# Slot attention stage of a transformer kernel: the first stage's instructions in another order

## What is computed

```python
q = _rope(x @ Wq); k = _rope(x @ Wk); v = x @ Wv          # x is the layer norm of the input
sk = clip(x @ sk_w1 @ sk_w2 + sk_b2, -32, 32)             # low rows (16), then slots' logits (4 x 64)
sv = clip(x @ sv_w1 @ sv_w2 + sv_b2, -32, 32)
wk = exp(sk); zk = cumsum(wk)
S = where(mask, q @ k.T, 0)
p = softmax(S @ wk * scale / zk)
wv = exp(sv); zv = cumsum(wv)
A = where(mask, (p / zv) @ wv.T, 0)
o = A @ v
g = x @ Wg
on = o * rsqrt(mean(o * o) + EPS) * gnorm_w
return x + (on * g * sigmoid(g)) @ Wo
```

## Time and profile before

| what | us |
|---|---|
| median of 3 runs | 1717.63 |
| lowest and highest of them | 1714.06, 1718.74 |
| the profiled execution's own time | 1717.68 |
| its span, first to last instruction | 1715.9 |
| of it the first stage | 306 |

### The profile page before, as it was taken

The page is one execution under the profiler, slowest core; times in us unless marked ns, Lnnn a source line. Parts: engine busy times, 40 slices in busy tenths (PEclk is TensorE's granted clock), DMA queues, the critical chain, the costliest instruction groups (busy, mean ns, idle before and its releaser), DMA issues. The chain is left out here.

```text
span 1715.9 us, 37883 instructions
## 1 busy us (share of the span) xinstructions
PE 1520.5 (89%) x14142; PEld 731.0 (43%) x14142; DVE 1189.5 (69%) x1931; ACT 1256.8 (73%) x2113; POOL 529.5 (31%) x908
## 2 busy tenths in 40 slices
PE   7899997784699999998889999968874999999998
PEld 4676665662133333336633333345541333333256
DVE  4677778798999999966710000048878999999743
ACT  4555553597488888885679999925763888888863
POOL 3432342552323333334400000013212233333362
PEclk9899989797699999999989999989986999999999
DMA  4000000025534343320133333201333333333211
GB/s 132 1 1 1 1 1 1 1 78 156 155 97 110 108 112 107 109 64 27 38 94 95 96 100 97 68 24 49 99 106 113 84 90 92 87 93 93 67 38 38
DMA packets 140410, 125.42 MB, mean 73 GB/s; under 512 B 38410, under 2 KB 118340, under 8 KB 140228
## 3 DMA queue, kind: packets, MB, share of 16 engines
q1 hardware_dynamic: 130980, 121.90, 23.9%
q0 software_dynamic: 8192, 0.77, 0.9%
q10 hardware_dynamic: 1056, 0.33, 0.1%
HBM read 77.19 MB, written 44.96 MB: 71 GB/s over the span
## 5 line engine op out<-in xcount | busy, mean ns | idle before, releaser
L1700 ACT ACTIVATE m_probs<-m_psum 128x512 f32<-128x512 f32 (+1 forms) x768 | 511.7, 762 | 63.1 <-PE m_psum L1623 62.2
L1700 ACT ACTIVATE e_probs<-e_psum 128x512 f32<-128x512 f32 x512 | 276.3, 596 | 53.3 <-PE e_psum L1623 51.8
L1740 DVE TENSOR_REDUCE a_minus_max<-m_psum 128x2 f32<-128x1024 f32 x256 | 300.9, 1219 | 14.3 <-PE m_psum L1632 13.0
L1740 DVE TENSOR_REDUCE a_minus_max<-e_psum 128x2 f32<-128x1024 f32 x256 | 300.6, 1219 | 14.4 <-PE e_psum L1632 13.0
L1623 PE MATMUL m_psum<-m_q_stack,m_k_stack 114*32 114x512 bf16 (+1 forms) x4096 | 295.8, 385 | 6.7 <-DMA m_k_stack<-n_parts 4.6
L1643 PE MATMUL m_psum<-m_probs,m_v_ones 128*32 128x512 f32 x2048 | 271.0, 602 | 3.4 <-DVE m_pair L1690 2.1
L1623 PEld LDWEIGHTS m_psum<-m_q_stack,m_k_stack 114*32 114x32 bf16 (+1 forms) x4096 | 106.9, 96 | 225.8 <-issue 126.2
L1623 PE MATMUL e_psum<-e_q_stack,e_k_stack 126*32 126x512 bf16 x2048 | 157.8, 385 | 2.2 <-ACT e_probs L1700 2.2
L1643 PE MATMUL e_psum<-e_probs,e_v_ones 128*32 128x512 f32 x1024 | 132.2, 593 | 0.0
L1632 PE MATMUL m_psum<-m_k_stack,m_q_stack 48*128 48x512 bf16 x512 | 93.0, 400 | 32.0 <-DVE a_minus_max L1740 24.4
L1632 PE MATMUL e_psum<-e_k_stack,e_q_stack 60*128 60x512 bf16 x512 | 93.9, 400 | 27.9 <-DVE a_minus_max L1740 22.6
(11 more groups left out here) (401 smaller groups left out, 2648.1 us busy)
## 6 DMA issues: line engine op xcount, KB each, us to landing
polar_q<-m_late SPq DMA_DIRECT2D x24, 256.0 KB, 3.0
polar_k<-m_late SPq DMA_DIRECT2D x24, 256.0 KB, 3.4
m_q_stack<-polar_q SPq DMA_DIRECT2D x64, 96.0 KB, 2.3
m_k_stack<-polar_k SPq DMA_DIRECT2D x64, 96.0 KB, 2.4
ctx<-a_context_pairs SPq DMA_DIRECT2D x48, 128.0 KB
a_context_pairs<-slot_w SPq DMA_DIRECT2D x24, 256.0 KB, 2.2
m_q_stack<-dist_parts SPq DMA_DIRECT2D x192, 32.0 KB
m_k_stack<-dist_parts SPq DMA_DIRECT2D x192, 32.0 KB
```

The lines of the kernel that those rows point to most:

```text
L1700: act.activation(self.buf.probs[(NT * m + c) % self.buf.PROBS][:, self.WIDE * part:self.WIDE * (part + 1), :], self.ps_s[i % self.PAIRS], ...
L1740: dve.tensor_reduce(self.minus_max[n % 2][:, k:k + NT + 1:NT], self.ps_r[r % self.TWOS], AX.X, ALU.max, negate=True).then_inc(self.two_fre ...
```

## The change

`gate_sigmoid` is cut into three methods, one for each activation, and the lists of PE, ACT and DVE are written in another order, with the banks' plan to match. On PE: `low` goes between the two `slot_logits`; the projections of tiles 3 and 2 follow those of 1 and 0 directly, ahead of `mean_squares` and `project_out`; `slot` 1 and 0 end the step with `gate` behind them; `slot` 2, `key_sums` 0 and `slot` 3 begin the next. The gate moves from bank 5 to bank 4, behind the contexts `o` and ahead of `xnT`. On ACT the four activations of the gate go into the next step, one by one between the copies for scores and `weights` 3. On DVE `clip` 1 and 0 come behind `apply_rms`, `scan` 1 ends the step ahead of `clip` 2, the statistics of the next sequence come earlier, and `gate_product` comes behind the second `state_copy`. POOL's list stays as it is. No operation is added or dropped.

```diff
-            ("slot2", 2, 1, ...), ("slot3", 3, 1, ...), ("zk0", 5, 1, ...),
+            ("slot2", 2, 1, ...), ("zk0", 5, 1, ...), ("slot3", 3, 1, ...),
...
-            ("low", 4, 0, ...), ("gT", 5, 0, (slot.gated_ready,)), ("slot1", 1, 0, ...), ("slot0", 0, 0, ...)
+            ("slot1", 1, 0, ...), ("slot0", 0, 0, ...), ("gT", 4, 0, (slot.gated_ready,))
...
                     for b in batch(s, 1):
-                        slot.qkv_copy(act, b, 2)
-                        slot.low_copy(act, b)
-                        slot.gate_guard(act, b)
-                        slot.gate_sigmoid(act, b)
-                        slot.weights(act, b, 1)
-                        slot.weights(act, b, 0)
+                        slot.weights(act, b, 2)
                     for b in batch(s, 2):
                         slot.exponential(act, b)
...
                     for b in batch(s, 1):
-                        slot.weights(act, b, 2)
                         slot.key_log(act, b, 0)
+                        slot.gate_guard(act, b)
+                        slot.k_copy(act, b)
+                        slot.gate_exponential(act, b)
+                        slot.q_copy(act, b)
+                        slot.gate_logarithm(act, b)
+                        slot.weights(act, b, 3)
+                        slot.gate_sigmoid(act, b)
                     for b in batch(s, 2):
                         slot.value_log(act, b)
-                    for b in batch(s, 1):
-                        slot.k_copy(act, b)
-                        slot.q_copy(act, b)
                     for b in batch(s, 0):
                         norm.normalise(act, b)
-                    for b in batch(s, 1):
-                        slot.weights(act, b, 3)
                     for b in batch(s, 2):
                         slot.value_inverse(act, b)
```

More of the change, by code:

```diff
@@ L2516, in _ @@
                         slot.slot(pe, b, 2)
+                        slot.key_sums(pe, b, 0)
                         slot.slot(pe, b, 3)
-                        slot.key_sums(pe, b, 0)
                         slot.states(pe, b, 1)
@@ L2543, in _ @@
                         slot.slot_logits(pe, b, 1)
+                    for b in batch(s, 0):
+                        slot.low(pe, b)
+                    for b in batch(s, 1):
                         slot.slot_logits(pe, b, 0)
@@ L2552, in _ @@
                         slot.turn_values(pe, b, 1)
+                    for b in batch(s, 0):
+                        slot.project(pe, b, 3)
+                        slot.project(pe, b, 2)
                     if s == LAST:
@@ L2562, in _ @@
                     for b in batch(s, 0):
-                        slot.project(pe, b, 3)
-                        slot.project(pe, b, 2)
-                        slot.low(pe, b)
-                        slot.gate(pe, b)
                         slot.slot(pe, b, 1)
                         slot.slot(pe, b, 0)
+                        slot.gate(pe, b)
                 folding.turn_ternary(pe, 0)
@@ L2608, in _ @@
                         norm.copy(act, b)
+                        slot.low_copy(act, b)
                     if s == LAST:
                         folding.keep_products(act)
+                    for b in batch(s, 0):
+                        slot.qkv_copy(act, b, 1)
                     for b in batch(s, 2):
@@ L2619, in _ @@
                     for b in batch(s, 0):
-                        slot.qkv_copy(act, b, 3)
-                        slot.qkv_copy(act, b, 0)
+                        slot.weights(act, b, 1)
+                        slot.weights(act, b, 0)
                 folding.finish_proj(act)
@@ L2648, in _ @@
                         slot.state_copy(dve, b, 2)
+                        slot.gate_product(dve, b)
                         slot.mask_scores(dve, b, 0)
@@ L2678, in _ @@
                         slot.subtract(dve, b)
+                    for b in batch(s + 1, 0):
+                        norm.statistics(dve, b)
+                        norm.aggregate(dve, b)
+                    for b in batch(s, 1):
                         slot.scan(dve, b, 0)
@@ L2681, in _ @@
                         slot.apply_rms(dve, b)
+                    for b in batch(s, 0):
+                        slot.clip(dve, b, 1)
+                        slot.clip(dve, b, 0)
+                    for b in batch(s, 2):
+                        slot.apply_gate(dve, b)
                     if s != LAST:
@@ L2684, in _ @@
                             slot.add(dve, b)
-                    for b in batch(s, 2):
-                        slot.apply_gate(dve, b)
+                    for b in batch(s, 1):
+                        slot.scan(dve, b, 1)
                 folding.finish_fc(dve)
```

35 lines of the change are left out of this document (17 added, 18 removed).

## The result

The changed kernel takes **1739.7 us** (median of 4, 1736.5 to 1742.8) beside 1718.1 for the kernel before on the same chip: a ratio of **1.0128**, 95% interval 1.0111 to 1.0145. Forecast were 1729.7 and at most 1738, so the time lies outside the range. The sign was right, and the loss, 21.6 us, is nearly twice the 12 that were forecast.

What follows compares the result with a forecast made beforehand. PE was taken to bound the stage, its clock second, with late `value_inverse` on ACT lengthening steps. Steps, start and end gave +9.8 us and the clock +2.2, together +12.0 on 1717.7: 1729.7 us, range 1711 to 1738.

Steps and rivals of the forecast that it cites:

- five steps, full clock: Steps between the attentions of steps 2 and 7: 35.35 us each against 34.14, five times +1.2, +6.0.
- step 8, full clock: Last step, without a normalisation on ACT: 33.8 us against 33.0, +0.8.
- drain: End of the stage behind step 8: the same chain on DVE as before, so no change.
- Piece one: Attention to the end of the projections on PE: 12.95 us instead of 14.36.
- piece two: End of the projections to `states` 1, set by POOL's rope: 10.1 us instead of 9.51.
- Piece three: `states` 1 to attention: later `value_inverse` on ACT delays `attend`, 12.3 us instead of 9.69.
- Rivals A and B: A: ACT not late, about 1711 us, chance 0.16. B: `value_inverse` later by 1.4 instead of 2.6, 1720.7, chance 0.18.
- DVE's tail: DVE's work up to `clip` 2, which releases `weights` 2: a us sooner there saves a us in each step.
- the pair on DVE and POOL: `apply_gate` on DVE newly meets POOL's rope and they exclude each other: 0.6 us more in a step.
- the clock term: Half clock in PE's new waits makes `turn_k` and ACT later by about 1.1 us: two steps taken, +2.2.
- rival C: Clock falls in the new waits in every step: 1734 us, 1738 with a second fall; chance 0.66 together with the forecast.
- the start term: First step: normalisation behind the gate and `weights` 3, logits some 1.9 us later, attention of step 2 some 3.

Runs made afterwards that it cites:

- e4_filled_waits: The changed kernel with the matmuls of `key_sums` 0 and both `turn_p` issued twice, in PE's waits, same output; 1729.7 us, ratio 1.0075 to the kernel before.
- e3_scan_back: The changed kernel with DVE's `scan` 1 back between `clip` 2 and `clip` 3, as in the kernel before; 1741.9 us, ratio 1.0139.
- f2_log_early_filled: f1_log_early with the matmuls of `key_sums` 0 and both `turn_p` issued twice; 1711.6 us, ratio 0.9959 to the kernel before.
- f1_log_early: The changed kernel with ACT's four gate activations together ahead of `weights` 2 and `value_log` ahead of `k_copy`; 1718.4 us, ratio 1.0000 to the kernel before.
- f3_low_late_once: The changed kernel with the first sequence's `low` and its copy put behind the projections, in the first step only; 1741.4 us, ratio 1.0120.
- h1_after_full_rows: The changed kernel with the slots' matmuls over 128 rows instead of 33, same result; 1740.4 us, ratio 1.0118 to the kernel before.
- h2_rows_one_fill: f1_log_early with 128 rows in the slots, `gate_product` between `clip` 2 and 3, and only `key_sums` 0 issued twice; 1708.4 us, ratio 0.9934.

## Why the prediction was right in sign and too small

The measured 1739.7 us lie above the upper end of the range, 1738. Two terms of the sum failed, the clock and the start; the three pieces held. Against e4_filled_waits, in which the clock is full from 54.5 to 296 us (so the fall at 50.5 to 54.5 is still in the start's term), the loss of the profiled execution in the stage splits into these terms. The drain is read from the changed kernel itself, since the duplicates lengthen it in e4_filled_waits:

| term of the sum | forecast | measured | from |
|---|---|---|---|
| five steps, full clock | +6.0 | +5.4 | 244.45 - 68.38 - 170.71 |
| step 8, full clock | +0.8 | +0.8 | 33.81 - 33.00 |
| start | +3 | +6.9 | 68.38 - 61.44 |
| drain | 0 | -0.1 | 45.98 - 46.05 |
| clock | +2.2 | +8.0 | 6.5 in the five steps, 0.9 in step 8, 0.6 in the start |
| sum | +12.0 | +21.0 | |

**Right: the bound and the three pieces.** Piece one was put at 12.95 us and measured 13.11, piece two at 10.1 and 9.78, two small errors that partly cancel. Piece three was put at 12.3 and measured 12.30 at full clock, in e4_filled_waits; in the changed kernel it is 12.4 to the last mask (`states` 1 at 238.19, the mask done at 250.24, some 0.3 to land). `value_inverse` was to end 8.3 behind `states` 1 and ended 8.41 behind; `over_sums` 1 was to wait 2 us or more for it and waited 2.21. Rivals A and B, ACT not late or half as late, are excluded by that row, and the half clock right behind the slots is gone, as foretold.

**Right with a wrong reason in it.** The prediction drove piece three from the start of `weights` 2 and named DVE's tail as its weakest point: a us there would be a us in each step. e3_scan_back made `clip` 2 earlier and won nothing. In the profile both chains, from `weights` 2 and from `turn_k`, meet at `k_copy` within 0.23 us, and so the sum came out right by either, which was luck. The one from `turn_k` is the one that a lower clock makes longer.

**Right: the pair on DVE and POOL.** The row of piece two shows the exclusion that was priced at 0.6:

```profile
229.33 5.44 POOL L1964 TENSOR_TENSOR s_rope_product<-s_qkv,rope 128x512 f32<-128x512 f32 x4 [23.70 <-ACT s_qkv L1923]
234.85 2.06 POOL L1969 TENSOR_TENSOR s_qk<-s_rope_product 128x512 f32<-128x512 f32 x1
236.88 1.26 POOL L1970 TENSOR_TENSOR s_qk<-s_rope_product 128x512 f32<-128x512 f32 x1
```

The products take 5.44 instead of 5.01, with `apply_gate` beside them at 0.75 instead of 0.68, and the subtraction 2.06 instead of 1.28, with `scan` 1 beside it; the addition is alone again, 1.26 instead of 2.19. So the new neighbour costs 0.43, and the scan 0.8, where it was 0.9. The Trainium skill's rule ("SBUF — State Buffer", section "Who interferes with whom") has it that way, an exclusive lock for a DVE instruction with two SBUF inputs, and the trace agrees, with 0.43 where 0.6 was taken.

**Wrong: the clock term, "between no such step and all six: 0 to 6.6; I take two, 2.2".** It fell in all of them, and in two steps twice. The bound was worked out right, 1.1 a step against 1.3 measured, and the value inside it was chosen without a row; rival C, priced at 1734 to 1738, came nearest and had been put down as a variant. The step that failed is this choice of how many steps have a fall: the term measured 8.0. The cheap fall behind the slots went, as foretold, and one or two dearer ones a step stand in its place. The prediction named the waits that would bring them and did not count them in every step. The mean clock from 60 to 275 us is 0.94 in both kernels: the changed one has no more half clock than the one before. In the kernel before, most of it lies behind the slots, ahead of a wait for the rope, and only the two steps in which it reached `states` 1 and `turn_k` are long (35.16 and 35.07 beside 33.4 to 33.6). In the changed kernel it lies at `turn_k` and the key sums, where every us is on the path.

**Wrong: the start term, "some 1.9 later, and the attention of step 2 some 3".** It measured 6.9. The logits of step 1 came 4.0 later, with or without the duplicates (36.36 in e4_filled_waits). Of that, 1.6 us had arisen at the first `states` 1 already (24.98 instead of 23.36), ahead of the normalisation to which the forecast put the whole of its 1.9. Behind the logits the forecast added 1.1 for what is in fact a whole step of the new kind, and 3.5 came (3.0 in e4_filled_waits). `low` now runs between the two halves of the logits, so the projections end 1.1 later behind them; both scans meet the rope (1.83 and 2.29 us, at 46.92 and 49.85), 0.5 more; and from `states` 1 to the attention it takes 13.16 us instead of 11.22. The five steps were counted from the attention of step 2 on, and the lengthening inside the step that leads to it was left out of the sum.

**Wrong, but small.** `key_sums` 1 was said to have its bank "before the masks are", without cost; it waits 0.67 for `over_sums` 1 in each step, and that wait is one of those ahead of the half clock at 247.5. The 0.82 ahead of the transposes of the next input (244.64) was not foreseen either, while the wait for the masks ahead of `attend`, foretold as one of the longest, is 0.56.

## What to carry to other kernels

A mean clock says how much half clock there is, not what it costs: mark where each fall stands, ask whether a wait hides it, and when an edit moves falls onto the path, let the range reach as far as a fall in every step. Here all six steps had one. When an engine's queue is late, look for the last thing it was released by: only work that is taken out from behind that point helps, and here two edits that brought its start forward won little or nothing. And count the first step as one of the steps.

## What was not expected of the hardware

- Work of no use in PE's waits made the changed kernel's first stage 6.1 us shorter (the median 10.0 us), and f2_log_early_filled 6.8 us faster than f1_log_early (5.8 in the stage), with the granted clock at 1.00 instead of 0.94 and 0.96 from 60 to 275 us. The same work made the kernel before 7.6 us slower and left its clock at 0.94.
- In the kernel before, matmuls over 128 rows instead of 33, at the same column count and nearly the same duration (3.60 us for the four slots instead of 3.70), raised the granted clock from 0.94 to 0.98. In these traces PE's busy share alone does not tell when it falls.
- The half clock held for 13.5 us with PE busy throughout (f3_low_late_once, 19.5 to 33.0).
- Executions of one kernel differ with their mean clock: 1734.2 us at 0.948 and 1745.1 at 0.936 (h1_after_full_rows). Steps without a fall do not make them alike: h2_rows_one_fill spreads by 1.8 us over five executions, f2_log_early_filled by 9.3 over ten.
